# Wide cross-attention layers: the normalised rows are turned ahead of the first keys, and the output bias is added in the fourth unit

## The reference

```
def _cross_attention(q_in, kv_in, wq, bq, wk, bk, wv, bv, wo, bo, bias_k, bias_v):
    qh, kh, vh = (q_in @ wq + bq), (kv_in @ wk + bk), (kv_in @ wv + bv)   # split in H heads of K
    kh = concatenate([kh, bias_k]);  vh = concatenate([vh, bias_v])       # one more key and value
    weights = softmax(einsum(qh, kh) / sqrt(K))
    return einsum(weights, vh) @ wo + bo
...
    h = _layer_norm(x, ln1_scale, ln1_offset)
    x = res + _cross_attention(h, xf_1, wq1, bq1, ...)
    h = _layer_norm(x, ln2_scale, ln2_offset)
    x = res + _cross_attention(h, xf_2, wq2, bq2, ...)
```

## Time and profile before

| | us |
|---|---|
| median of 3 runs | 1101.68 (1100.23 to 1102.01) |
| profiled execution, its own time | 1103.04 |
| its span, first to last instruction | 1101.2 |
| mean granted TensorE clock | 0.936 of full |
| TensorE matmuls, busy | 954.1 (87%) |
| VectorE, busy | 782.7 (71%) |
| ScalarE, busy | 604.4 (55%) |
| Pool, busy | 312.4 (28%) |

### The profile page before, as it was taken

How to read it: one execution, slowest core, us unless ns; L and a number is a source line. 1 busy time by engine, 2 the same in 40 slices (tenths; PEclk the granted TensorE clock), 3 DMA queues, 4 the chain that set the end, 5 groups by cost and what they waited for, 6 DMA issues and landing times. The chain is left out here.

```text
span 1101.2 us, 17924 instructions
## 1 busy us (share of the span) xinstructions
PE 954.1 (87%) x6616; PEld 808.7 (73%) x6616; DVE 782.7 (71%) x1627; ACT 604.4 (55%) x1369; POOL 312.4 (28%) x321
## 2 busy tenths in 40 slices
PE   4889886779999999997889999998678799779958
PEld 4666665667988889887778898888557566566647
DVE  3486766367787878787578787787594688567864
ACT  3587873134555555553355565555353688277851
POOL 3454540040112222221102222110003456344520
PEclk8899997878999999999799999999978899789989
DMA  4995006130001111110001111000023930294020
GB/s 140 271 231 87 1 1 237 28 138 1 34 7 39 39 40 39 39 37 22 20 1 39 40 39 39 1 1 1 21 99 99 240 62 1 83 242 72 5 83 20
DMA packets 39490, 72.71 MB, mean 66 GB/s; under 512 B 6534, under 2 KB 23944, under 8 KB 37228
## 3 DMA queue, kind: packets, MB, share of 16 engines
q1 hardware_dynamic: 39404, 71.56, 24.2%
HBM read 55.28 MB, written 16.27 MB: 65 GB/s over the span
## 5 line engine op out<-in xcount | busy, mean ns | idle before, releaser
L1308 ACT CAST L1a_probsT_hi<-L1a_bank 128x512 fp32r<-128x512 f32 x128 | 68.8, 589 | 94.2 <-PE L1a_bank L1189 94.2
L1147 POOL TENSOR_SCALAR L1a_wo_hi<-L1a_stage 128x512 fp32r<-128x512 f32 x16 | 10.7, 670 | 362.5 <-PE L1a_sums L74 356.1
L1425 DVE TENSOR_REDUCE L1a_top<-L1a_scores 128x2 f32<-128x1024 f32 x64 | 78.2, 1222 | 36.1 <-PE L1a_scores L74 36.1
L1340 ACT ACTIVATE L1a_probs<-L1a_scores,L1a_neg_max 128x512 f32<-128x512 f32 x128 | 86.9, 684 | 30.2 <-DVE L1a_bias_shifted L1429 25.2
L1363 DVE TENSOR_TENSOR L1a_probsT_lo<-L1a_bank,L1a_probsT_hi 128x512 fp32r<-128x512 f32 x128 | 82.0, 682 | 0.1
L72 PE MATMUL L1a_bank<-L1a_probsT_hi,L1a_v_hi 128*128 128x256 f32 x256 | 73.1, 286 | 9.2 <-DVE L1a_probsT_lo L1363 9.2
L1310 ACT ACTIVATE L1a_attended_hi<-L1a_bank,L1a_cols 128x256 fp32r<-128x256 f32 x64 | 30.5, 476 | 90.4 <-PE L1a_bank L74 90.4
L72 PE MATMUL L1a_bank<-L1a_w_hi,ctxT_hi 128*128 128x256 f32 x256 | 76.6, 299 | 0.0
L73 PE MATMUL L1a_bank<-L1a_w_lo,ctxT_hi 128*128 128x256 f32 x256 | 73.8, 288 | 0.0
L417 POOL TENSOR_SCALAR L0a_probs<-L0a_probs,L0a_inverse 128x768 f32<-128x768 f32 x64 | 57.2, 906 | 58.7 <-DVE L0a_inverse L686 58.7
L74 PE MATMUL L1a_bank<-L1a_w_hi,ctxT_lo 128*128 128x256 f32 x256 | 73.8, 288 | 0.0
(11 more groups left out here) (410 smaller groups left out, 3106.3 us busy)
## 6 DMA issues: line engine op xcount, KB each, us to landing
L1a_stage<-in_L_w SPq DMA_DIRECT2D x15, 1024.0 KB, 4.8
L0m_fold_wq<-in_L_wqT SPq DMA_DIRECT2D x2, 2048.0 KB, 13.0
L0a_k_dram<-L0a_kT_hi SPq DMA_DIRECT2D x8, 384.0 KB, 10.6
L0a_k_stack<-L0a_k_dram SPq DMA_DIRECT2D x4, 576.0 KB
L0a_w_qkv<-L0a_k_dram SPq DMA_DIRECT2D x4, 576.0 KB
L0a_wide_wo<-in_L_wo SPq DMA_DIRECT2D x1, 2048.0 KB, 16.6
L0a_wide_wo<-in_L_wo SPq DMA_DIRECT2D x2, 1024.0 KB, 17.7
L0m_stage<-in_L_wm SPq DMA_DIRECT2D x4, 512.0 KB, 6.5
```

Source lines behind the costliest of these rows:

```text
L1308: nc.scalar.copy(out, source).then_inc(ring.hi_done, 1)
L1340: nc.scalar.activation(probs[:, g % 2, qt, :], scores[:, qt, :], ACT.Exp, bias=neg_max[:, g % 2, qt:qt + 1], accum_out=row_sum[:, g % 2, q ...
L1425: link(nc.vector.tensor_reduce(top[:, :], scores[:, :, :], AX.X, ALU.max))
```

## The change

In the first layer's `START` the two transposes stand ahead of the keys. TensorE turns the rows before it waits for the first weights; ScalarE scales them after its first weight conversion; VectorE splits them after its first weight split. In the second layer this order stays (`n == 3 and layer`). ScalarE and VectorE wait for `cols_scaled` only ahead of the queries, and TensorE ahead of the bias scores. VectorE does both column products, then both scalings. The output bias is no longer added ahead of the first k_lo; in both layers it is added in the fourth unit (`gl == 3`), ahead of the low part of the attended rows. Pool waits for the job `norm1` to be emptied before it splits anything.

```
-        START = KV[:4] + ["norm0", "norm1"] + KV[4:] + QS + ["bias_scores"]
+        START = ["norm0", "norm1"] + KV + QS + ["bias_scores"]
...
             parts[0].root(nc, pool)
+            ring.wait_evacuated(pool, job_of["norm1", 0])
             for p in range(ALL):
...
-                pe.wait_ge(bias_ready, layer + 1)
+                pe.wait_ge(cols_scaled, LAYERS)
+                pe.wait_ge(ones_set, 2)
...
                 if layer:
                     pe.wait_ge(w_ready, PAIRS + 1)
+                else:
+                    parts[layer].transpose(nc, pe, ring, keep)
...
-                    if n == 3:
+                    if n == 3 and layer:
                         parts[layer].transpose(nc, pe, ring, keep)
...
                               1.0 if c else scale).then_inc(first_hi, 1)
+                if c == FIRST_ORDER[0]:
+                    parts[0].scale(nc, act, ring)
             act.wait_ge(small_loaded, 48 * LAYERS)
-            act.wait_ge(cols_scaled, LAYERS)
...
-                    if n == 3:
+                    if n == 3 and layer:
                         parts[layer].scale(nc, act, ring)
+                act.wait_ge(cols_scaled, LAYERS)
                 for item in QS:
...
                         low_weights(n + 1, c)
+                        if n == 0:
+                            split_norm(layer)
                     dve.wait_ge(small_loaded, 48 * LAYERS)
                     for i in range(LAYERS):
-                        link(nc.vector.tensor_tensor(bias_product[i][:, :], cols[i][:, 0, :], cols[i][:, 1, :], ALU.mult))
+                        last = nc.vector.tensor_tensor(bias_product[i][:, :], cols[i][:, 0, :], cols[i][:, 1, :], ALU.mult)
+                    link(last)
+                    for i in range(LAYERS):
                         nc.vector.tensor_scalar(cols[i][:, 0, :], cols[i][:, 0, :], scale, None, ALU.mult).then_inc(cols_scaled, 1)
-                    dve.wait_ge(cols_scaled, LAYERS)
                     dve.wait_ge(ones_set, 2)
-                dve.wait_ge(parts[layer].normed_ready, 1)
-                for t in range(RT):
-                    last = nc.vector.tensor_tensor(keep["x"][:, t, :], keep["x"][:, t, :], out_bias[layer][:, :], ALU.add)
-                last.then_inc(bias_ready, 1)
...
-                    if n == 3:
+                    if n == 3 and layer:
                         split_norm(layer)
+                dve.wait_ge(cols_scaled, LAYERS)
                 for item in QS:
...
                             low(job_of[p + 1, item], destination(p + 1, item), bias_of(p + 1, item))
+                    if gl == 3:
+                        dve.wait_ge(parts[layer].normed_ready, 1)
+                        for t in range(RT):
+                            last = nc.vector.tensor_tensor(keep["x"][:, t, :], keep["x"][:, t, :], out_bias[layer][:, :], ALU.add)
+                        link(last)
                     if gl:
```

More of the change, by code:

```diff
@@ L1096, in wide_attentions @@
         first_loaded = [ph.sem(f"first_loaded{c}") for c in range(4)]
-        first_hi, first_lo, ones_set, bias_ready = ph.sem("first_hi"), ph.sem("first_lo"), ph.sem("ones_set"), ph.sem("bias_ready")
+        first_hi, first_lo, ones_set = ph.sem("first_hi"), ph.sem("first_lo"), ph.sem("ones_set")
         block = ph.block()
```

## The result

| | before | changed |
|---|---|---|
| median | 1101.85 us (1100.23 to 1106.34, 4 runs) | 1090.82 us (1088.89 to 1090.92, 4 runs) |
| changed / before | | 0.9887, 95% interval 0.9872 to 0.9902 |
| profiled execution, its span | 1103.04 us, 1101.2 us | 1090.92 us, 1089.1 us |
| mean granted TensorE clock | 0.936 | 0.944 |

The change makes the kernel 11.0 us faster; the forecast was 1090.6 us in a range of 1088.0 to 1093.5.

A forecast was written before the change was run, and what follows sets the result against it. The prediction took TensorE, busy 87% of the span, as the bound, so only its waits counted. Gains of 9.8 (first layer) and 1.4 (second), less 0.1 (additions), took 1101.68 to 1090.6 us; range 1088.0 to 1093.5.

The forecast's parts named there:

- (1) Transposes and split: First layer's start: transposes ahead of the keys start at 218.04, keys at 219.64, turned rows split by 222.26.
- (2) Keys: First layer's start: keys from 219.64 are done at 226.1 or 226.9, depending on when the clock rises.
- two cases: First layer's keys: clock rises at 221.56 as before, or 5.2 us after TensorE starts.
- step (3): First layer's start: column work costs nothing; k_lo starts at 225.65 instead of 232.19, values at about 226.7.
- (4) Bias scores: First layer: bias scores start at 235.2 instead of 244.99, gaining 9.8 us, bounds 9.5 and 10.1.
- lower bound of 9.5: Smallest gain in us forecast for the first layer's bias scores, with values at 226.9 and 8.6 us to follow.
- (5) What is late next: First layer: scores still 5.49 us after bias scores start; Pool has 1.1 us to spare, each further us counts.
- Pool is late: Rival, chance 0.03: Pool's chain in the first start exceeds its spare 1.1 us by 2 to 4: 1093 to 1095.
- Second layer: Second layer's start: without additions ahead of k_lo, transposes start at about 522.16 instead of 523.56, gaining 1.4 us.
- The rival in which the clock survives the wait: Rival, chance 0.25: TensorE's clock stays full through the second layer's 3.2 us wait, 2.0 us more gained: 1088.6.
- The additions: Fourth unit of both layers: moved additions are nearly covered by VectorE's gaps, costing 0.04 us per layer, 0.1 in all.
- The sum: Whole kernel: 9.8 + 1.4 - 0.1 = 11.1 us gained, giving 1090.6 us.

The follow-up runs named there:

- after_again: The changed kernel, unedited, measured again on another chip: 1088.54 us, ratio 0.9868 to the kernel before.
- e6: The changed kernel with VectorE's two column products and two scalings moved ahead of its second weight split: 1088.16 us, ratio 0.9875 to the kernel before.
- e5: The changed kernel with Pool waiting for the fourth key's bank instead of the turned rows: 1088.36 us, ratio 0.9873 to the kernel before.
- e7: The changed kernel with the negated bias scores written by ScalarE from PSUM instead of by VectorE: 1084.59 us, ratio 0.9838 to the kernel before.
- e9: The changed kernel with the four additions moved from the fourth unit to the sixth, beside Pool's weight splits: 1093.03 us, ratio 0.9901 to before.
- e1: The changed kernel with the four additions put back ahead of the first k_lo, new order kept: 1102.76 us, ratio 1.000 to the kernel before.
- e4: The changed kernel with four further additions, never read, behind the four in each fourth unit: 1090.78 us, ratio 0.9894 to the kernel before.
- e3: The changed kernel without Pool's new wait for the turned rows: 1089.69 us, ratio 0.9887 to the kernel before.
- e2: The changed kernel with the old order and without Pool's wait, additions staying in the fourth unit: 1093.83 us, ratio 0.9926 to before.

## Why the prediction came out right, step by step

**(1) Transposes and split: right.** Relative to the phase's start the transposes stood at 4.66 us (forecast 218.04 - 213.29 = 4.75), the keys at 6.28 (6.35), the split ended at 8.90 (8.97).

**(2) Keys: right, a little early.** The clock rose at about 219.4, 2.8 us after TensorE's start, before either of its two cases (3.5 and 5.2 us); the keys were through and the wait ahead of the values began at 224.47, 12.6 us into the phase (12.8 to 13.6). With k_lo late by step (3), this left a wait of 1.08 us where the prediction said that there would be none; it was 0.3 in after_again.

**(3) The scaled columns: right in sign, too cheap.** k_lo started at 12.78 (forecast 12.36), because the second weight split itself came at 9.55 instead of 8.89: it waited 0.64 us for ScalarE's conversion of weights that had arrived later. In after_again it was 11.97. So this is the spread of a transfer, and the 0.4 us is a term that the range, not the sum, should carry. What I did not see is what the columns' place beside Pool costs by itself: e6 shows 1.5 us of VectorE, of which little reaches TensorE.

**(4) Bias scores: 9.46 us gained, forecast 9.8** (31.70 - 22.24). The values followed k_lo by 0.88 us (forecast 0.89) and took 8.58 us (8.5) to the bias scores: the clock stayed up, as the step said. All of the 0.34 us is step (3)'s; just under the lower bound of 9.5.

**(5) What is late next: the size right, the reason wrong.** 5.49 us from bias scores to scores, in this kernel as before, and Pool had 1.25 us to spare (234.45, idle before) where I read 1.1. But "each further us would be on the path" is wrong beyond the first: e5 shows the opposite, Pool 4.5 us later made the scores 2.8 us earlier. I had read the earlier trace rows as a chain, last query, Pool's split, negation, scores. The middle link is no dependency: the negation needs nothing of Pool's. The rival "Pool is late" (2 to 4 us beyond the spare time) was priced with the wrong sign at e5's lateness, 3.2 us beyond it. For a small lateness the sentence may still hold: Pool's long instruction began 1.16 us before the negation (236.01 and 237.17), so by this reading up to about 1.2 us beyond the spare time would still be paid in full. That is an estimate from these two rows; no run has it. The same misreading hid the largest gain that these runs found in this stretch, e7's.

The Trainium skill (SBUF — State Buffer, section "SBUF: two separate sides") calls the pair of ports that VectorE and Pool share an exclusive lock that goes to whoever starts first, for a whole instruction. The traces agree for the negation, which started behind Pool's instruction: it took 2.31 us and ended at 239.48 with Pool's 236.01 + 3.42 = 239.43, and took 0.20 in a gap of Pool's (e5). They don't agree in e9: there Pool's instruction has the earlier start on record, by 0.03 us, and it was the one held, through four instructions of VectorE.

**Second layer: 1.44 us at the transposes, forecast 1.4** (10.02 - 8.58). 0.36 of it went again: the clock came back at about 516.35, 6.0 us after TensorE's restart at 510.35; in the kernel before it was 5.2. The rival in which the clock survives the wait did not happen in this profile: TensorE stopped at 507.20, the clock fell at about 509.5, inside a wait of 3.15 us. In after_again, with the transposes at the same place (8.56), the clock was back 3.0 us after the restart and the second start 1.3 us shorter (24.95).

The rival did happen in e9, whose second start is that of the changed kernel: TensorE stood 3.13 us ahead of the transposes, the granted clock stayed at 1.00, and eight transposes took 1.22 us instead of 1.94. The bias scores came at 18.40 instead of 20.69, 2.3 us earlier, where the rival had said 2.0. e9, TensorE, and two stretches behind it:

```profile
511.38 1.22 PE L775 MATMUL L1a_bank<-ident,L1a_normed 128*128 128x128 f32 x8 [3.13 <-DVE L1a_k_lo L1371]
```

```profile
508.00:512.00 4.00, 0.87 (x7) 0.47 (x5) 4.00 (x7) 0.69 (x1) 1.95 (x3) 1.00 0.42 109
512.00:516.00 4.00, 4.00 (x33) 3.76 (x33) 3.86 (x7) 2.25 (x4) 0.00 (x0) 1.00 0.37 156
```

e9's edit touches nothing in this start, so the difference is put down to the execution. Of the twelve profiles with the shortened wait (all but before and e1) this is the one in which the clock stayed up.

**The additions: right in size, by a misread unit.** The earlier trace rows show gaps of 1.09 and 0.40 us and say that they are the fourth unit's. They are the fifth's: the maxima (L1425) count the units, and 275.13 is the fourth. What the additions go ahead of stands at 281.53 in the kernel before:

```profile
281.53 0.48 DVE L1365 SCALAR_TENSOR_TENSOR L1a_attended_lo<-L1a_bank,L1a_cols,L1a_attended_hi 128x256 fp32r<-128x256 f32 x1 [0.64 <-ACT L1a_attended_hi L1310]
282.82 1.22 DVE L1425 TENSOR_REDUCE L1a_top<-L1a_scores 128x2 f32<-128x1024 f32 x1 [0.80 <-PE L1a_scores L74]
```

0.64 + 0.80 = 1.44 us against 1.49: the same by chance. And the comparison of added work with gaps was too strict: e4 put 2.9 us into gaps of 1.44 and lost 0.8 us at most in a layer, where the comparison would give 1.5.

**Not foreseen: 0.91 us in the first layer's units.** Behind the first scores the clock was at half for 3.4 us (it fell at 239.87, 0.25 us after TensorE had resumed, and rose at 243.28), in the kernel before for 5.2 (250.48 to 255.69, it had fallen during the stop), though TensorE's stop ahead of them was the same (2.75 and 2.74 us). Half of the 1.8 us difference is 0.9, which is all of it. This is spread, not an effect of the change: after_again gained 0.54 (4.5 us at half), e3 0.14 (5.2).

**The sum.** Forecast 9.8 + 1.4 - 0.1 = 11.1; measured 9.46 + 1.08 + 0.91 - 0.19 = 11.26. Two terms were 0.3 too high and one gain came in that was not in the sum. The second profile of the same kernel gives 10.28 + 2.42 + 0.54 + 0.05 = 13.3. The terms hold to a few tenths where they rest on an instruction's place and to 1 to 2 us where they rest on the clock.

## What to carry to other kernels

When two engines end at the same moment, ask what the later one needs of the other; here it needed nothing and was only held while the other worked, and moving that one small instruction to ScalarE brought the scores of two layers forward by 4.3 us together. Small SBUF-to-SBUF instructions on VectorE that sit in the chain to TensorE (additions, column scalings, a negation) belong where Pool is idle, or on ScalarE reading PSUM. Judge a reordering together with what it clears: the new order alone was worth nothing that a median shows, the moved additions alone two thirds, and the last third came mostly from keeping a split off Pool's time. Before a few tenths between two profiles are explained, take out the time at half clock: it differed by more than 2 us between executions of the same start.

## What the runs showed of the hardware that was not expected

- A chain of VectorE instructions can hold Pool as well as be held: the same four additions took 6.62 us beside Pool in one place and 1.42 in another, where Pool's instruction grew from 1.30 to 2.58.
- Size is no protection: instructions on 128x2 elements took 0.16 us alone and 2.10 (L1433 in e5) or 2.01 us (L1442 in e9) beside Pool's split, while four k_lo of 128x512 with an operand in PSUM took 2.71 to 2.73 in the kernels before and changed, e1 and e2, each with Pool at work beside them, and the same 2.71 in the second layer (509.46 in the changed kernel), where Pool is idle.
- The clock fell also behind a wait of only 0.5 us (e7: granted clock 0.58 from 238 to 240 us, TensorE busy for all of it), where ahead of the wait stood 2.7 us of matmuls with 16 columns each (234.21 to 236.95). The shorter wait did not keep the full clock there, so e7's gain is that of its two stalls. In the second start of e9 it stayed full through a wait of 3.13 us behind matmuls of 512 columns; what made the difference was not tested.
